# Five short stages retimed: norm copies on two engines, angles and the bias term moved back, three values pieces moved forward

## The reference, cut to what matters

```python
x += cross_attention(layernorm(x), context)              # 8 heads, plain
x += delta_rule_attention(layernorm(x))                  # 4 heads of 64, chunks of 32 tokens
x += mixture_of_experts(layernorm(x))                    # 15 experts, best 3, and a shared one
x += cross_attention(layernorm(x), context, bias=fside)  # 16 heads, biased
x += quantised_attention(layernorm(x))                   # 8-bit rounding of weights and activations
x += recurrent_cell(layernorm(x))                        # one step per batch row
```

## Time and profile before

| | us |
|---|---|
| median of the 3 timed runs (1903.51 to 1905.51) | 1905.01 |
| the profiled execution | 1906.91 |
| its span, first to last instruction | 1905.1 |
| TensorE matmuls busy | 1832.0 |
| VectorE busy | 1541.2 |
| ScalarE busy | 861.9 |
| GpSimd busy | 927.4 |

### The profile page before, as it was taken

One profiled execution on the slowest core, in us unless ns is written; L12 is line 12 of the kernel. 1 busy time (PEld: TensorE's weight loads), 2 busy tenths in 40 slices (PEclk: granted clock), 3 DMA queues, 4 the chain that ended last, 5 costly groups with the idle time before them and its releaser, 6 DMA issues. The chain is left out here.

```text
span 1905.1 us, 45489 instructions
## 1 busy us (share of the span) xinstructions
PE 1832.0 (96%) x17954; PEld 1250.4 (66%) x17965; DVE 1541.2 (81%) x2137; ACT 861.9 (45%) x1205; POOL 927.4 (49%) x440
## 2 busy tenths in 40 slices
PE   8999999999879899999999999999999999999788
PEld 5667666666647689766666666666666676667545
DVE  4666766676777666799999999999999999999784
ACT  3666666666633345244343334443444344434401
POOL 0356655665652144045575557555755475547300
PEclk9999999999889789999999999999999999999889
DMA  3000110000030232000000000120000000000100
GB/s 141 10 15 0 52 65 14 0 14 9 7 140 3 82 116 72 12 10 15 0 14 14 14 0 14 48 70 7 7 14 14 8 6 14 14 8 2 39 13 12
DMA packets 27778, 52.64 MB, mean 28 GB/s; under 512 B 4260, under 2 KB 15285, under 8 KB 27189
## 3 DMA queue, kind: packets, MB, share of 16 engines
q1 hardware_dynamic: 27232, 51.34, 8.2%
q10 hardware_dynamic: 468, 0.16, 0.0%
HBM read 50.97 MB, written 0.52 MB: 27 GB/s over the span
## 5 line engine op out<-in xcount | busy, mean ns | idle before, releaser
L363 POOL TENSOR_TENSOR biased_sums<-biased_sums,biased_scores 128x1024 f32<-128x1024 f32 x216 | 512.7, 2374 | 138.5 <-ACT biased_scores L670 119.1
L736 DVE TENSOR_TENSOR biased_scores<-ps,bias 128x1024 f32<-128x1024 f32 x256 | 312.5, 1221 | 35.2 <-PE ps L451 33.8
L750 DVE TENSOR_TENSOR ps<-ps,biased_scores 128x512 f32<-128x512 f32 x480 | 334.7, 697 | 4.5 <-DVE ps L750 0.5
L757 DVE TENSOR_TENSOR biased_scores<-biased_scores,ps 128x1024 f32<-128x1024 f32 x256 | 306.6, 1217 | 3.5 <-PE ps L509 2.8
L670 ACT ACTIVATE biased_scores<-biased_scores 128x1024 f32<-128x1024 f32 x256 | 263.0, 1052 | 97.4 <-DVE biased_scores L757 95.3
L363 POOL TENSOR_TENSOR plain_sums<-plain_sums,plain_scores 128x1024 f32<-128x1024 f32 x104 | 246.5, 2370 | 60.6 <-ACT plain_scores L670 50.2
L750 DVE TENSOR_TENSOR ps<-ps,plain_scores 128x512 f32<-128x512 f32 x240 | 167.4, 697 | 118.1 <-ACT plain_scores L653 113.2
L451 PE MATMUL ps<-biased_queries,keys_again 64*128 64x256 f32 x2048 | 257.3, 391 | 3.9 <-DVE biased_scores L736 3.2
L463 PE MATMUL ps<-biased_scores,biased_values 128*64 128x256 f32 x2048 | 245.3, 382 | 3.6 <-ACT biased_scores L670 3.2
L398 PE MATMUL ps<-weights_again,context_again 128*64 128x128 f32 x4096 | 248.1, 274 | 0.0
L398 PEld LDWEIGHTS ps<-weights_again,context_again 128*64 128x64 f32 x4096 | 228.6, 137 | 28.7 <-issue 17.9
(11 more groups left out here) (413 smaller groups left out, 2201.4 us busy)
## 6 DMA issues: line engine op xcount, KB each, us to landing
moe_w<-in_moe_w SPq DMA_DIRECT2D x32, 256.0 KB, 2.8
weights_again<-in_wqkv SPq DMA_DIRECT2D x45, 128.0 KB, 2.2
context<-in_ctx_t SPq DMA_DIRECT2D x4, 1024.0 KB, 6.7
context_again<-in_ctx_t SPq DMA_DIRECT2D x4, 1024.0 KB, 7.5
bias<-in_fside SPq DMA_DIRECT2D x1, 4096.0 KB, 14.6
biased_w_out<-in_w_out SPq DMA_DIRECT2D x16, 256.0 KB, 2.6
context<-in_ctx_t SPq DMA_DIRECT2D x2, 1536.0 KB, 8.9
context_again<-in_ctx_t SPq DMA_DIRECT2D x2, 1536.0 KB, 9.8
```

The source lines that it names most:

```text
L363: pool.tensor_tensor(both(SUM[:, :, :, :]), both((E[:, 0] if kp == 1 else SUM)[:, :, :, :]), both(E[:, kp, :, :, :]), ALU.add).then_inc(su ...
L736: dve.tensor_tensor(E[:, kp, :, :, :].rearrange("p (h t) n j -> p h t (n j)", h=2), scores_bank(kp).rearrange("p (h t n) -> p h t n", h=2, ...
L750: ins = dve.tensor_tensor(to, highest, E[:, kp, :, n, :], ALU.max)
L757: dve.tensor_tensor(at, at, c.ps[:, LOWER, :].rearrange("p (a j) -> p a j", a=HQ).unsqueeze(2) .to_broadcast([P, HQ, 2, P]), ALU.add).then ...
```

## The change

1. **Norm rows by two engines.** In the delta and recurrent stages VectorE copies the first half of XNT and ScalarE the second; `ln_ready` counts to 2 for each stage. In the experts ScalarE takes the high part of x straight from PSUM, half by half, and VectorE copies the halves of XNT beside it. In the quantised stage VectorE reduces each half from PSUM, and ScalarE makes both copies.
2. **Delta.** The angles are multiplied behind the convolutions. `next_keys` becomes `next_piece`: eleven pieces, eight of keys and three of values of the first biased pair, begin in TensorE's waits for silu; values go into a buffer that is allocated ahead of the stage. The last of them stands between the turned k and the turned kb. At the end three matmuls are streamed ahead of the output product, and the late tiles are turned between products.
3. **Experts.** TensorE begins with the first hidden layer and computes the router behind it; hidden layers and outputs of the first two pairs alternate from there. VectorE splits the first hidden part of expert 0, GpSimd that of expert 1. The bias term goes to the end of the stage. The loads of the second pair go ahead of the load of the attention bias.
4. **Biased first sweep.** It has three values pieces less and an order of its own.

```diff
+def norm_first_half_turned(c, dve, k, bank=0):
+    dve.wait_ge(c.ln_turned, k + 1)
+    dve.tensor_copy(c.XNT[:, 0, :], c.ps[:, bank, :]).then_inc(c.ln_ready, 1)
+def norm_second_half_turned(c, act, k, bank=0):
+    act.wait_ge(c.ln_turned, k + 1)
+    act.activation(c.XNT[:, 1, :], c.ps[:, bank + 1, :], ACT.Copy).then_inc(c.ln_ready, 1)
...
+EARLY_VALUES = 3
+FIRST_BEFORE_SCORES = {4: ("V", 4), 6: ("V", 6), 7: ("V", 7)}
+FIRST_AFTER_SCORES = {0: ("K", 0), 1: ("K", 1), 2: ("V", 3), 3: ("K", 2), 4: ("K", 3), 5: ("V", 5), 7: ("K", 4)}
...
# delta, TensorE
                 for s in range(3):
-                    keep_streaming(c, pe, (7, 4, 0)[s], 1)
+                    next_piece(s)
                     pe.wait_ge(silu_done, s + 1)
...
+                for n in range(3, BEFORE_VALUES + 2):
+                    next_piece(n)
                 pe.wait_ge(gamma_rows, T)
+                pe.wait_ge(piece_kept, KEYS_BEFORE + BEFORE_VALUES)
...
-                for g in range(5):
-                    next_keys(g)
-                pe.wait_ge(v_ready, M)
-                for g in range(5, KEY_PIECES):
-                    next_keys(g)
+                for n in range(BEFORE_VALUES + 2, NEXT_PIECES - 1):
+                    next_piece(n)
                 for bank, rows, ready, count in ((4, K, k_ready, 1), (6, KB, k_ready, 2), (0, Q, q_ready, 1)):
                     if bank == 6:
-                        pe.wait_ge(piece_kept, KEYS_BEFORE + KEY_PIECES)
+                        next_piece(NEXT_PIECES - 1)
+                        pe.wait_ge(piece_kept, KEYS_BEFORE + NEXT_PIECES - 2)
+                    elif bank == 0:
+                        pe.wait_ge(piece_kept, KEYS_BEFORE + NEXT_PIECES)
...
+                keep_streaming(c, pe, 3, 3)
                 for n, t in enumerate((0, 2)):
                     project_o(t, n + 1)
-                for n, t in enumerate(LATE_TILES):
                     pe.wait_ge(o_ready, n + 1)
-                    turn_o(t)
+                    turn_o(LATE_TILES[n])
...
# delta, VectorE
-                dve.wait_ge(mix_done, 1)
-                st.add(dve.tensor_scalar(KEEP[:, :], MIX[:, :], -1.0, 1.0, ALU.mult, ALU.add))
-                for kind in range(2):
...
                 dve.wait_ge(w_in, 16 * 2)
                 for s in range(3):
                     dve.wait_ge(lin_done, s + 1)
...
+                dve.wait_ge(mix_done, 1)
+                st.add(dve.tensor_scalar(KEEP[:, :], MIX[:, :], -1.0, 1.0, ALU.mult, ALU.add))
+                for kind in range(2):
...
# experts, TensorE
-                keep_streaming(c, pe, 5)
+                keep_streaming(c, pe, 9)
...
-                        for n, (w, x) in enumerate(TERMS):
+                        for n, (x, w) in enumerate(TERMS):
+                            if first and n == 2 and j == 0:
+                                pe.wait_ge(x_low, 1)
...
+                pe.wait_ge(x_high, 2)
+                hidden_sums(0, 0, True)
+                pe.wait_ge(c.ln_ready, 2 * (k + 1))
+                route()
+                hidden_sums(0, 1)
+                outputs(0, 0)
                 next_hidden(1, 0)
-                pe.wait_ge(added, T)
+                pe.wait_ge(exps, T)
+                outputs(0, 1)
                 next_hidden(1, 1)
                 next_outputs(1, 0)
...
+                turn_shares()
                 next_outputs(E // 2 - 1, 1)
+                output_bias()
...
# quantised attention, VectorE
-                norm_vector_turned(c, dve, k)
-                dve.wait_ge(c.ln_ready, k + 1)
-                column(0, c.XNT[:, :, :].rearrange("p j n -> p (j n)")).then_inc(col, 1)
+                dve.wait_ge(c.ln_turned, k + 1)
+                column(2, c.ps[:, 0, :]).then_inc(half_reduced, 1)
+                dve.wait_ge(c.ln_ready, 2 * k + 1)
+                column(3, c.ps[:, 1, :]).then_inc(half_reduced, 1)
+                dve.wait_ge(half_reduced, 2)
+                dve.tensor_reduce(COL[:, 0:1], COL[:, 2:4], AX.X, ALU.max).then_inc(col, 1)
# quantised attention, TensorE
-                pe.wait_ge(c.ln_ready, k + 1)
+                pe.wait_ge(c.ln_ready, 2 * (k + 1))
+                pe.wait_ge(half_reduced, 2)
                 gather(1, 0, 6)
```

254 lines of the change are left out of this document (159 added, 95 removed).

## The result

| | before | changed |
|---|---|---|
| median, us (lowest to highest, 5 runs each) | 1904.29 (1903.51 to 1905.51) | 1890.46 (1889.08 to 1897.49) |
| the profiled execution | 1906.91 | 1889.08 |
| its span | 1905.1 | 1887.3 |

The ratio is 0.9939, 95% interval 0.9926 to 0.9952: faster by 0.6%, 11.6 us, with 9.5 forecast (the medians in the table alone lie 13.8 apart). The two profiled spans are 17.8 us apart, and that is too much for the edits. I cut every profile into stages at VectorE's first statistics of each norm.

What follows compares the result with a forecast made beforehand. TensorE, busy 96% of the span, bounds the kernel; the edited short stages have it waiting. Delta 3.35, experts 4.9, biased sweep 1.1, quantised −0.1, recurrent 0.3 sum to 9.55 us: 1895.5 for the timed median, range 1891.5 to 1901.

Steps and rivals of the forecast that it cites:

- (a): Delta: VectorE and ScalarE copy 512 columns of XNT each, so the products start 0.5 us sooner.
- (b): Delta: convolutions wait for the first product, not the angles; rotations start 3.8 us sooner by VectorE alone.
- (c): Delta: ScalarE is late next, so its root for k comes 3.2 us sooner, not 3.8.
- (d): Delta: the eleventh piece, 1.89 us, stands on TensorE between turned k and kb; grams start 2.85 us sooner.
- (e): Delta's tail: three streamed matmuls and late tiles turned between products gain 0.5 us, bounds 0 and 1.7.
- (f): Experts: TensorE starts with hidden(0,0), not the router; outputs(1,0) start 7.6 us sooner, with one slow clock stretch kept.
- (g): Experts: the bias term moved to the end of the stage costs 2.7 us there.
- 1 (more clock): Experts without a slow stretch behind the router, delta's state loop at 2.4 GHz: 1891.8 us; chance 14%.
- Rival 2: Delta: the moved angles wait for GpSimd's scaling at the SBUF port, +1.3 us, 1896.8; chance 10%.
- Rival 3: Experts stay slow: TensorE gaps behind the router and the second 1.2 GHz stretch returns; 1899.7 us; chance 12%.
- Rivals 4: Delta gives nothing: convolutions wait for something else and the pieces push the grams back; 1899 us; chance 6%.
- rival 5: First biased sweep: TensorE, less busy, falls to 1.2 GHz and stays, 29 us more, 1924.5 us; chance 4%.

Runs made afterwards that it cites:

- old_delta: Changed kernel with the delta stage and first biased sweep of before; median 1895.62 us, ratio 0.9959 to the kernel before.
- angles_early: Changed kernel with angles and mixing weights loaded earlier and the angles multiplied ahead of the first convolution; median 1891.85 us, ratio 0.9937 to the kernel before.
- after_again: The changed kernel run and profiled once more, without an edit; median 1891.84 us, ratio 0.9937 to the kernel before.
- router_first: Changed kernel with the experts' router ahead of the first hidden layer again; median 1898.90 us, ratio 0.9970 to the kernel before.
- before_again: The kernel before, run and profiled once more, without an edit; median 1904.81 us, ratio 1.0003 to itself.
- old_recurrent: Changed kernel, in whose recurrent stage VectorE alone copies the norm's rows again; median 1893.70 us, ratio 0.9943 to the kernel before.

## Why the prediction was right, step by step

The sign, the size within about 2 us of 11.6, and the experts ahead of delta as the largest parts were right. The median itself, 1890.46, is 1 us below the low end of the range, 1891.5; 11.6 off the 1905.01 that the forecast started from is 1893.4, inside it. By stage, with the profiles of the same code averaged, the parts are 5.4 for the experts (111.6 in three profiles with the old form, 106.2 in nine with the new one), 2.8 for delta, 1.5 for the recurrent stage and 0.9 for the sweep: about 10.5 of the 11.6. By step:

- **(a) halves of the norm rows.** 0.5 us forecast; 0.5 to 0.6 in the one place where it was undone alone (the recurrent stage), where I had taken 0.3. In delta the first product began 5.95 and 5.98 behind the stage's start before, and 5.4 or 6.5 after. At like clock it is 0.5: with eight transposes in 1.04 us it is 5.97 and 5.40, with 1.80 and 1.91 it is 6.99 in old_delta and 6.49.
- **(b) angles behind the convolutions.** 3.8 by VectorE; 4.0 when undone. Right.
- **(c) ScalarE is late next.** Right in the changed kernel's profile, shown by angles_early; VectorE by 0.48 in after_again. The size was too large: k is normalised 45.5 and 45.0 behind the stage's start before, 41.5 to 43.7 in six profiles after, 2.4 sooner on average with 3.2 forecast. The sentence that failed is the one that gave the moved keys pieces no price: where the first of them ran at 1.2 GHz, k came 1.1 later. That it is this piece that holds the rest up fits ten profiles, but no run took it away alone.
- **(d) the eleventh piece.** The other term that was mis-sized. I gave it 1.89 and bounded it at 2.3. It takes 1.95 at 2.4 GHz in four profiles of nine, and 3.21 to 3.44 in five, where the clock falls behind TensorE's wait of 1.9 us for k. The same wait (1.9, and 2.5 in after_again) stands ahead of the piece where it takes 1.95 too, so what decides is not shown. From router_first, with a granted clock of 0.50 from 580 to 582:

```profile
578.89 3.39 PE L1117 MATMUL ps<-weights_again,context_again 128*128 128x128 f32 x16
```

The trace of before could have warned me: a wait of 1.38 and then slow matmuls stand in the earlier trace rows, at the tail. From the normalising of k to the grams it is 7.6 us on average of the six, with 6.5 before: 1.1 dearer, with 0.35 forecast. The grams began 52.04 and 51.55 behind the stage's start before, and 49.90 to 52.07 in the six profiles of the new delta, 50.5 on average: 1.3 us, not 2.85. I had written that a start less than 1.5 us sooner would show me wrong; the first two profiles gave 1.55 and the average lies under it.
- **(e) the tail.** 0.5 forecast, bound 1.7; measured 2.57 between the first two profiles, 1.7 when the streaming alone was undone, 1.5 on average (7.0 in three profiles of the old form, 5.5 in the six). The reordering is the 0.5 that I took for it; the clock, which I all but left out, came on top. The errors in (c) and (d) and the one in (e) cancel, and that is luck: delta as a whole took 118.92 and 116.25 before (118.32 in old_delta), 117.8 on average, and 115.0 on average of six with the edits: 2.8, with 3.35 forecast.
- **(f) the experts' start.** hidden(0,0) began 6.28 behind the stage's start, with 6.4 forecast. outputs(1,0) came 8.7 us sooner than in the first profile of before, with 7.6 forecast with the slow stretch and 9.3 without, but 6.6 sooner than in before_again, which has one slow stretch in place of two. In the new form the clock went both ways, and it made no difference. In old_delta, whose experts are the changed kernel's, the slow stretch is there, right behind the router:

```profile
662.55 4.61 PE L1799 MATMUL ps<-moe_x_parts,moe_w_parts 128*128 128x512 f32 x12
...
678.34 3.04 PE L1810 MATMUL ps<-moe_w_parts,moe_hidden_parts 128*128 128x256 f32 x24
```

4.61 for 2.9 is the 1.7 that I had put down for it, yet outputs(1,0) come 28.37 behind the stage's start, no later than with full clock (28.44): at full clock TensorE waits 1.18 for VectorE instead. Five profiles of the new form have one such stretch and 28.37 to 28.77, three have none and 28.44 to 28.54. The end that I named, VectorE 0.9 ahead of its use, is the bound. That my sum was 1.1 too long has a plain cause: I added busy times (2.91, 3.0, 3.5) where the starts of successive groups are 2.75, 2.88 and 3.37 apart; the end of a group overlaps the next.
- **(g) the bias term at the end.** 2.7 forecast, 2.0 measured, for the same reason, and for 1.99 in place of 2.35 at full clock.
- **Biased sweep.** 1.1 forecast; 1.2 between the first two profiles, 0.9 on average (0.5 to 1.2), VectorE without gaps in half of the profiles and clock 1.00, as said. TensorE's busy time was 37.9, not 35.2; a busy row counts what is in the pipeline, so the values pieces that left probably didn't take their whole busy time with them.
- **Quantised stage.** The first rounded product starts 6.82 behind the transposes for 6.65: 0.17 later, with 0.1 forecast.
- **Recurrent.** 0.3 forecast, 1.5 measured: 0.5 for the halves and 1.0 that I can't explain.

Of the rivals, 1 (more clock) came true in part: no slow stretch in the experts in the profiled run, a tail at 2.4 GHz, but the state loop kept its low clock, 0.50 to 0.56 from its first to its last state matmul in all fourteen profiles. Rival 2 is false where I put it: the angles took 1.70, four of the eight beside GpSimd's scaling and the others beside its addition. It holds for other instructions, below. Rival 3 shows in part in one profile, that of old_recurrent, with clock 0.87, a hidden layer of 5.49 us, no wait, and outputs(1,0) at 29.75, 1.3 us late. Rivals 4 and 5 didn't happen. What I held against rival 5 was one-sided: the trace of before also has stretches of 5 us with 4.1 to 4.2 busy where the clock is 0.66 (from 1775), 0.84 (from 680) and 0.86 (from 1805).

## What to carry to other kernels

Profile each version more than once, or take all its variants together, before a stage's difference is read as the edit's: here 4.7 of 17.8 us lay in a stage that no edit touched. Put extra work into a wait, not behind it, and price it at the slow clock as well: the piece that stood just behind a wait met the slow clock in five profiles of nine and cost 1.7 times its price. When an engine is relieved, look at who is late next before crediting it: 2.6 us taken off VectorE's list bought nothing by itself. With ScalarE's and TensorE's lists changed too delta was 1.9 shorter; which part of that the angles brought wasn't separated.

## What the runs showed of the hardware

A VectorE instruction with two SBUF inputs and a GpSimd instruction beside it held each other up, and in the rows below the one that began later lost. One instruction of the experts' rank work in the changed kernel, then GpSimd's two subtractions beside it:

```profile
666.65 2.07 DVE L1945 TENSOR_TENSOR moe_greater<-moe_greater,moe_equal 128x900 f32<-128x900 f32 x1
```
```profile
665.62 2.14 POOL L1717 TENSOR_TENSOR moe_hidden_parts<-moe_hidden,moe_hidden_parts 128x512 fp32r<-128x512 f32 x1
667.72 2.16 POOL L1898 TENSOR_TENSOR moe_w_parts<-moe_w,moe_w_parts 128x512 fp32r<-128x512 f32 x1
```

The same instruction in old_delta, and GpSimd's subtraction beside it:

```profile
669.04 1.10 DVE L1914 TENSOR_TENSOR moe_greater<-moe_greater,moe_equal 128x900 f32<-128x900 f32 x1
```
```profile
669.13 2.16 POOL L1686 TENSOR_TENSOR moe_hidden_parts<-moe_hidden,moe_hidden_parts 128x512 fp32r<-128x512 f32 x1 [2.21 <-ACT moe_hidden_parts L1731]
```

In old_delta VectorE began 0.09 us ahead and took 1.10; GpSimd ended 1.15 behind VectorE's end, and takes 1.3 elsewhere in the stage. In the changed kernel GpSimd had begun first: VectorE ended 0.95 behind GpSimd's end, and GpSimd's next one 1.17 behind VectorE's. The gate rows did it too: 2.46 beside GpSimd's two-input additions in the changed kernel, 0.56 beside its scaling in angles_early. A one-input scaling of GpSimd that had begun 0.76 us before let the first four products of the angles pass at full speed, but the normalising of k at 1.90 in place of 1.22 ran beside one that began 0.14 after it. The Trainium skill, SBUF — State Buffer, section "SBUF: two separate sides", says that such a pair excludes each other for a whole instruction and that the one that starts first has it. The rows above agree; the angles and the normalising of k don't.
